# Softmax attention on one core: when the numerator products of the first exponential tile are issued

## The chip, the cores and the metric

The kernel runs on one NeuronCore of one Trainium2 chip. The metric is the device time of one launch in microseconds (us). Engines are named as the profile names them: PE is TensorE, PEld its weight loads, DVE is VectorE, ACT is ScalarE, POOL is GpSimd, SP is SyncE.

## What is computed

Four layers follow each other on x of shape 8 x 512 x 512: a cosine attention, a ternary feed-forward block, a softmax attention and a channel mix. The change touches only the third:

```python
# x is 8 x 512 x 512 here, context 8 x 512 x 384, N_HEADS = 16, HEAD = 32
q = x @ w_q + b_q
k = context @ w_k + b_k
v = context @ w_v + b_v
scores = jnp.einsum('bqhd,bkhd->bhqk', q, k) * scale
weights = jax.nn.softmax(scores, axis=-1)
out = jnp.einsum('bhqk,bkhd->bqhd', weights, v).reshape(B, Lq, D)
return out @ w_o + b_o
```

The "numerators" are the products of exp(scores) with v before the division by the row sums.

## The kernel before

`softmax_attention` runs over 8 batches; each has four head groups (m = 0 to 3) of four heads of 32 columns. A head group is worked in 16 units u. Unit u = 4t + h is head h and key tile t of 128 keys: one score matmul of 128 keys x 512 queries (`score`, L1779), and one exponential on ACT (`exponential`, L1497) into a slot of E. Four units with the same t make one exponential tile. I call the stretch of PE's order that begins with such a tile "block t".

E has twelve slots of 512 columns for sixteen exponentials: `SLOT = (0, 4, 8, 4)`, so tile 3 takes the slots of tile 1. Before that, POOL adds tile 1 onto tile 0 and later tile 3 onto tile 2 (`summed`, L1381), and PE multiplies the sums by ones to have the softmax denominators (`denominators`, L1795).

Each engine runs its own fixed list in order, and semaphores tie the lists together. On PE each block t is, for all groups but the very last:

1. `maxima` of the next head group, query tile t (L1761): four matmuls into PSUM banks 0 to 3. They wait until ACT has read the four scores of the block before, since scores use the same banks.
2. `attend(b, m, t - 1)` (L1787): the numerators of the exponential tile before, four heads beside each other in four column groups, into the bank `NUM`. It signals `s_pv`. Block 0 instead takes tile 3 of the group before, and its first denominators.
3. In block 1 (in block 2 for m = 3) the second denominators of the group before.
4. Scores u = 4t to 4t + 3, with projections, value products, transposes and output products (`between`) put between them by tables. The scores with h = 0 and h = 2 wait (`s_red`) for DVE: it has to reduce the maxima in banks 0 and 1, then those in banks 2 and 3 (`maxima` on DVE, L1626, two instructions for each block), before the banks may be written again.

The semaphore `s_pv` has these readers that matter here. On POOL, `summed(b, m, 0, i)` waits for the numerators of tile 0 (count 16m + 4), because it writes over what they read. On ACT, the exponentials of tile 1 wait for the group before, and those of tile 3 for the numerators of tile 1 (16m + 8) and for `summed`. `attend(b, m, 0)` itself waits for `s_av`: ACT has copied the group before out of `NUM` (`numerators`, L1503). POOL's order in a group is: two sums of the group before, the low part of the next query projection, `summed(b, m, 0, 0)`, then (by m) the division remainder, the low key part, the small normalisation steps, and `summed(b, m, 0, 1)`.

Of the kernel before, what the change touches and what calls it, by code (L numbers as in the profile page):

```python
# [1183 lines left out]
def softmax_attention(env, ctx_d, bq_d, bk_d, wv_d, bv_d, wo_d, bo_d, wr_d, wkk_d, mur_d, muk_d):  # L1184
# [31 lines left out]
    with ExitStack() as ctx:  # L1216
# [78 lines left out]
        def what(b, m, first, last):  # L1295

            return (None if last and m + 2 >= NG else group(b, m, 2),
                    None if last and m + 1 >= NG else group(b, m, 1),
                    (b, m - 1) if m else None if first else (b - 1, NG - 1),
                    (b, m - 2) if m >= 2 else None if first else (b - 1, NG + m - 2))  # L1300
# [413 lines left out]
        def _(e):  # L1714
# [11 lines left out]
            def queries(b, m, w, c, bank=None):  # L1726
                bank = bank or (7 if w else q_bank(m))
                n, k, xh, xl = (("q", KD, zh, zl), ("k", KC, ch, cl))[w]
                if c == 0:
                    if m == 0:  # L1730
                        (s_zl, s_cl)[w].wait(e, b, (KD, 1)[w])
                    if bank in reader:
                        take(bank)
                    reader[bank] = (s_qkf, b, 2 * m + w + 1)
                cols = lambda x: lambda c: x[n][:, c * D + m * P:c * D + (m + 1) * P]
                last = product(banks[bank][:, :], cols(wh), cols(wl), lambda c: xh[:, c, :], lambda c: xl[:, c, :], c, k)
                if c == k - 1:
                    last.then_inc(s_p.sem, 1)

            def values(b, m, t, i=None):  # L1740
                begin = i is not None
                i = i if begin else v_bank(m)
                if t == 0 and not begin:
                    take(i)
                    reader[i] = (s_V, b, m + 1)
                rows = lambda x: lambda c: x[:, c, t * P:(t + 1) * P]
                cols = lambda x: lambda c: x["v"][:, c * D + m * P:c * D + (m + 1) * P]
                for c in range(KC):
                    last = product(banks[i][:, t * P:(t + 1) * P], rows(ch), rows(cl), cols(wh), cols(wl), c, KC)
                if t == TT - 1:  # L1750
                    last.then_inc(s_vp.sem, 1)

            def maxima(b, m, q):
                if q == 0:
                    e.wait_ge(s_qkh.sem, s_qkh.count(b, 2 * m + 2))
                    s_mrow.wait(e, b, m)
                s_red.wait(e, b, 2 * (TT * m + q))
                high = qkh[m % 2]
                for h in range(4):
                    head = slice(h * DH, (h + 1) * DH)  # L1760
                    last = e.matmul(MX[h][:, :], high[head, 0, q * P:(q + 1) * P], high[head, 1, :], start=True, stop=True)  # L1761
                last.then_inc(s_mx.sem, 1)

            def rows(b, m):
                s_ex.wait(e, b, 16 * m - 3)
                e.wait_ge(s_red.sem, s_red.count(b, 2 * TT * (m + 1)))
                e.transpose(MX[0][0:4 * TT, 0:P], mx[:, :, :].rearrange("p h q -> p (h q)"), ident[:, :]).then_inc(s_mT.sem, 1)
# [14 lines left out]
            def attend(b, m, t):  # L1782
                if t == 0:
                    s_av.wait(e, b, m)
                e.wait_ge(s_ex.sem, s_ex.count(b, 16 * m + 4 * t + 4))
                for h in range(4):
                    e.matmul(NUM[h * DH:(h + 1) * DH, :], V[:, m, t, h * DH:(h + 1) * DH], E[:, SLOT[t] + h, :],  # L1787
                             start=(t == 0), stop=(t == TT - 1)).then_inc(s_pv.sem, 1)

            def denominators(b, m, p):  # L1790
                if p == 0:
                    s_an.wait(e, b, m)
                e.wait_ge(s_sum.sem, s_sum.count(b, 4 * m + 2 * p + 2))
                for h in range(4):
                    e.matmul(DEN[h * DH:(h + 1) * DH, :], ones[:, 0:DH], E[:, SLOT[2 * p] + h, :], start=(p == 0), stop=(p == 1))\  # L1795
                        .then_inc(s_dn.sem, 1)

            def transposed(b, c, end=False):
                if c == 0:
                    s_z.wait(e, b, TT)  # L1800
                take(7)
                chunk(e, b, c, R7)
                reader[7] = (s_zh if end else s_zl, b, c + 1)

            def output(b, q, c, i=6, end=False):
                if end:
                    e.wait_ge(s_al.sem, s_al.count(b, c + 1) + (q if c == NG - 1 else 0))
                elif q == 0:
                    s_al.wait(e, b, c + 1)
                if c == 0:  # L1810
                    if i < 4:
                        e.wait_ge(s_red.sem, s_red.count(b, 2 * TT * NG))
                        e.wait_ge(s_ex.sem, s_ex.count(b, 16 * (NG - 1)))
                    else:
                        take(i)
                    reader[i] = (s_res, b, q + 1)
                rows = lambda x: lambda c: x[:, c, q * P:(q + 1) * P]
                cols = lambda x: lambda c: x["o"][:, c * D:(c + 1) * D]
                last = product(banks[i][:, :], rows(ath), rows(atl), cols(wh), cols(wl), c, NG)
                if c == NG - 1:  # L1820
                    last.then_inc(s_o.sem, 1)

            def step(b, m, first, last):
                proj, nxt, div, late = what(b, m, first, last)
                if m == 0:
                    reader[6], reader[7] = ((s_qkf, b, 3), (s_qkf, b, 4)) if first else ((s_V, b, 1), (s_V, b, 2))

                def between(u):
                    if m == 1 and u in T_AT:
                        transposed(b + 1, T_AT.index(u), last)  # L1830
                    if proj:
                        for c in range(KD):
                            if Q_AT[m][c] == u and (u >= 0 or c):
                                queries(*proj, 0, c)
                        for c in range(KC):
                            if K_AT[m][c] == u:
                                queries(*proj, 1, c)
                    if not first:
                        for q, c in O_AT[m].get(u, ()):
                            output(b - 1, q, c)  # L1840
                    for n, when in V_AT[m].items():
                        for t in range(TT):
                            if when[t] == u and not (last and m == 3):
                                values(b + (m == 3), n, t)
                    if last and m == NG - 1 and u in END_UNITS:
                        q = END_UNITS.index(u)
                        for c in range(2):
                            output(b, q, c, END_BANK[q], True)

                if proj and Q_AT[m][0] < 0:  # L1850
                    queries(*proj, 0, 0)
                rows(b, m)
                if first and m == 1:
                    e.wait_ge(s_lo, 2)
                between(-1)
                for u in range(UNITS):
                    t, h = divmod(u, 4)
                    if nxt and h == 0:
                        if t == 0:
                            s_mrow.wait(e, b, m + 1)  # L1860
                        e.wait_ge(s_ex.sem, s_ex.count(b, 16 * m + 4 * t))
                        maxima(*nxt, t)
                    if t and h == 0:
                        attend(b, m, t - 1)
                    if div and u == 0:
                        attend(*div, TT - 1)
                        denominators(*div, 0)
                    if div and u == 4 * DN_TILE[m]:
                        denominators(*div, 1)
                    between(u - 0.5)  # L1870
                    score(b, m, u, nxt)
                    between(u)
# [28 lines left out]
            first_maxima(3, 0)  # L1901
            first_maxima(3, 1)
            steps(step, e)
            denominators(B - 1, NG - 1, 0)
            for h in range(4):
# [330 lines left out]
```

## Time and profile before

| | us |
|---|---|
| median of 3 runs | 1631.55 |
| lowest and highest of them | 1624.54 and 1632.25 |
| the profiled execution, its own time | 1632.94 |
| its span in the trace | 1631.0 |
| softmax attention, first to last score | 638.7 to 1329.7 in the span |
| one batch of it in the steady loop | 86.13 |

The profiled execution's time is 1.9 us more than its span, which is what lies around the span. To read the profile for this change, one looks at one batch of the softmax stage, since six of the eight batches repeat each other, and in it at the blocks t = 1 and t = 2 of each head group: when the maxima start, when the scores can follow, and when the next maxima start. In the timelines a row is start, duration, engine, line, operation with output and inputs, count; in brackets the idle time before it and what ended it. Rows that follow each other at once on one line are merged into one with their count; a numerator block is x8, since each of its four fp32 matmuls has two passes. Starts of matmuls are as recorded; they overlap, so PE's cost of a matmul is the distance to the next start and not its duration.

### The profile page before, as it was taken

Reading aid. Unit: us, or ns where it says so; the run is one execution under the profiler, and the core shown is the slowest. Engines: PE = TensorE matmul, PEld = TensorE weight load, DVE = VectorE, ACT = ScalarE, POOL = GpSimd, SP = SyncE. Lnnn points to the kernel's source line nnn. Section 1 sums busy time; section 2 is a strip of 40 time slices with the busy share of each in tenths; the row PEclk is TensorE's granted clock in tenths of the full one; section 3 lists DMA queues with packets and bytes.
Section 4 is the critical chain, followed back from the end, with each engine's and each line's share of the span. In section 5 each row is a group of like instructions: output and inputs, shape, how many; then the busy total and the mean of one; then the engine's idle time right before and its main releaser. Section 6 shows DMA issues by size and latency. Waiting matters only on the chain. (4 is left out here: it accounts for less than half of the span.)

```text
span 1631.0 us, 28525 instructions
## 1 busy us (share of the span) xinstructions
PE 1486.4 (91%) x8732; PEld 661.3 (41%) x8732; DVE 1219.0 (75%) x1468; ACT 1114.5 (68%) x1895; POOL 1049.1 (64%) x764
## 2 busy tenths in 40 slices
PE   5999887998999987889999999999999977999898
PEld 3545433444444433334343434343434323444343
DVE  4979899988989795667686868676777767665653
ACT  6667598788888764667676667666666656665563
POOL 4777536666776735667666767677767656556662
PEclk9989999999999998999999999999999988999999
DMA  8311000000000013221211212121211112232221
GB/s 322 141 65 65 1 1 1 1 1 1 0 0 1 1 66 95 55 57 37 57 38 42 56 35 58 34 58 35 57 36 40 56 35 44 52 85 66 55 52 52
DMA packets 91706, 79.52 MB, mean 49 GB/s; under 512 B 45792, under 2 KB 71264, under 8 KB 91104
## 3 DMA queue, kind: packets, MB, share of 16 engines
q1 hardware_dynamic: 88416, 69.70, 15.3%
q10 hardware_dynamic: 3200, 8.79, 1.4%
q8 instruction: 36, 0.59, 0.2%
q14 instruction: 54, 0.44, 0.1%
HBM read 37.40 MB, written 8.39 MB: 28 GB/s over the span
## 5 line engine op out<-in xcount | busy, mean ns | idle before, releaser
L1626 DVE TENSOR_REDUCE s_mx<-bank 128x2 f32<-128x1024 f32 x248 | 291.7, 1218 | 161.0 <-PE bank L1761 160.2
L1497 ACT ACTIVATE s_E<-bank 128x512 f32<-128x512 f32 x512 | 281.3, 597 | 167.4 <-PE bank L1779 166.1
L1381 POOL TENSOR_TENSOR s_E<-s_E 128x1024 f32<-128x1024 f32 x126 | 297.9, 2375 | 83.0 <-ACT s_E L1497 82.2
L1779 PE MATMUL bank<-s_QA,s_KA 97*128 97x512 f16 x512 | 164.8, 386 | 15.9 <-DVE s_mx L1626 12.5
L1787 PE MATMUL bank<-s_E,s_V 128*32 128x512 f32 x1024 | 138.6, 614 | 4.1 <-ACT s_E L1497 2.3
L796 POOL TENSOR_TENSOR sm_wkv<-sm_wkv,sm_cx 128x511 f32<-128x511 f32 x48 | 66.0, 1375 | 91.8 <-DVE sm_wkv L986 82.4
L1099 PE MATMUL bank<-sm_zz,w1raw 128*128 128x512 f16 x256 | 100.6, 393 | 25.7 <-DVE sm_cx L986 13.3
L1122 PE MATMUL bank<-f_w2q,w2raw 128*128 128x512 f16 x512 | 121.8, 379 | 0.6 <-DVE w2raw L974 0.3
L1630 DVE RECIPROCAL bank<-bank 128x256 f32<-128x256 f32 (+1 forms) x66 | 112.7, 1708 | 8.9 <-PE bank L1795 5.4
L790 POOL TENSOR_TENSOR w1raw<-w1raw,sm_cx 128x512 f32<-128x512 f32 x88 | 115.6, 1334 | 2.3 <-ACT sm_cx L878 2.3
L1989 POOL TENSOR_TENSOR sm_cx<-m_xf,sm_cx 128x512 f16<-128x512 f32 x60 | 82.4, 1393 | 42.2 <-ACT sm_cx L2048 42.2
L1099 PE MATMUL bank<-sm_wq,w1raw 128*128 128x512 f16 x256 | 97.2, 380 | 12.0 <-DVE sm_cx L986 7.7
L1100 PE MATMUL bank<-sm_zz,w1raw 128*128 128x512 f16 x256 | 100.4, 392 | 0.0
L1100 PE MATMUL bank<-sm_wq,w1raw 128*128 128x512 f16 x256 | 97.0, 379 | 0.0
L1779 PEld LDWEIGHTS bank<-s_QA,s_KA 97*128 97x128 f16 x512 | 41.1, 97 | 115.5 <-DVE s_mx L1626 74.9
L2096 DVE SCALAR_TENSOR_TENSOR m_xf<-sm_zz,sm_mu,m_part 128x512 f32<-128x512 f32 x60 | 59.9, 1024 | 28.6 <-ACT m_part L2040 28.6
L1122 PEld LDWEIGHTS bank<-f_w2q,w2raw 128*128 128x128 f16 x512 | 50.0, 98 | 61.2 <-ACT w2raw L936 0.8
L1374 POOL TENSOR_TENSOR sm_cx<-s_qkf,sm_cx 128x512 f16<-128x512 f32 x31 | 37.8, 1220 | 57.0 <-ACT sm_cx L1475 56.6
L1374 POOL TENSOR_TENSOR sm_cx<-s_qkf,s_qkh 128x512 f16<-128x512 f32 x32 | 37.1, 1159 | 58.0 <-ACT s_qkh L1475 57.7
L2156 PE MATMUL bank<-m_wvh,m_kh 128*128 128x512 f16 x128 | 49.7, 388 | 22.7 <-DVE m_y L2112 16.8
L1722 PE MATMUL bank<-sm_wkv,sm_cx 128*128 128x128 f16 x384 | 70.2, 220 | 0.0
L1724 PE MATMUL bank<-sm_wkv,sm_cx 128*128 128x128 f16 x384 | 69.8, 220 | 0.0
(280 smaller groups left out, 4095.4 us busy)
## 6 DMA issues: line engine op xcount, KB each, us to landing
sm_cx<-in_ctx SPq DMA_DIRECT2D x16, 768.0 KB, 4.6
X<-in_x SPq DMA_DIRECT2D x8, 1024.0 KB, 6.6
s_QA<-sm_cx SPq DMA_DIRECT2D x256, 32.0 KB, 1.9
out_x<-X SPq DMA_DIRECT2D x8, 1024.0 KB, 4.5
s_KA<-sm_cx SPq DMA_DIRECT2D x244, 32.0 KB, 1.9
w1raw<-in_w ACTq DMA_DIRECT2D x1, 4096.0 KB, 15.9
w2raw<-in_w ACTq DMA_DIRECT2D x1, 4096.0 KB, 29.5
s_QA<-s_qkh SPq DMA_DIRECT2D x128, 32.0 KB, 1.8
```

Of the source, the lines that this page charges most:

```text
L790: e.tensor_tensor(o, o, s2b[:, :], ALU.mult).then_inc(s_u.sem, 1)
L1099: e.matmul(hb(odd, j), w1q[:, cols], zh(odd, c), start=(c == 0), stop=False)
L1100: last = e.matmul(hb(odd, j), w1q[:, cols], zl(odd, c), start=False, stop=(c == KD - 1))
L1122: last = e.matmul(OB[q][:, :], whole16[:, r % NQ, q * P:(q + 1) * P, 0], w2q[:, ORDER[r] * D:(ORDER[r] + 1) * D], start=False, stop=(r == ...
L1374: e.tensor_tensor(qkl[:, w, :], f, qkh[m % 2][:, w, :], ALU.subtract).then_inc(s_qkl.sem, 1)
L1381: e.tensor_tensor(into, into, other, ALU.add).then_inc(s_sum.sem, 1)
L1497: e.activation(E[:, SLOT[k] + h, :], s_bank(u, nxt)[:, :], ACT.Exp, scale=1.0 / float(np.sqrt(DH)))\
L1626: e.tensor_reduce(mx[:, 2 * i:2 * i + 2, q], MAXED[i][:, :, :], AX.X, ALU.max).then_inc(s_red.sem, 1)
L1630: e.reciprocal(DEN[:, i * n:(i + 1) * n], DEN[:, i * n:(i + 1) * n]).then_inc(s_rc.sem, 1)
L1779: e.matmul(s_bank(u, nxt)[:, :], KA[0:MROW + 1, m, h, t * P:(t + 1) * P], QA[0:MROW + 1, m, h, :], start=True, stop=True).then_inc(s_sc.se ...
L1787: e.matmul(NUM[h * DH:(h + 1) * DH, :], V[:, m, t, h * DH:(h + 1) * DH], E[:, SLOT[t] + h, :], start=(t == 0), stop=(t == TT - 1)).then_in ...
L1989: e.tensor_tensor(xl[:, i, :], xf[:, i % 3, :], xh[:, i, :], ALU.subtract).then_inc(s_xl.sem, 1)
```

## The change

In the list of PE, no numerators are issued in block 1 any more; those of tile 0 are issued in block 2, ahead of those of tile 1. Block 3 keeps those of tile 2, and block 0 of the next group those of tile 3.

```diff
-                    if t and h == 0:
-                        attend(b, m, t - 1)
+                    if h == 0:
+                        for k in ((), (), (0, 1), (2,))[t]:
+                            attend(b, m, k)
```

The lists of the other engines are as they were. On PE, block 1 of head group m = 2 in the batch loop: ahead of the change the numerators of tile 0 stand between the maxima and the denominators (s_E with s_V is a numerator product, s_E with ones a denominator product).

```order
L1761 MATMUL bank<-s_qkh 128x512 [waits s_red,s_ex]
L1761 MATMUL bank<-s_qkh 128x512 x3
L1787 MATMUL bank<-s_E,s_V 32x512 [waits s_ex,s_av]
L1787 MATMUL bank<-s_E,s_V 32x512 x3
L1793 REGISTER_ALU
L1795 MATMUL bank<-s_E,ones 32x512 [waits s_sum]
L1795 MATMUL bank<-s_E,ones 32x512 x3
L1776 REGISTER_ALU
L1779 MATMUL bank<-s_QA,s_KA 128x512 [waits s_red]
```

The same place after the change:

```order
L1761 MATMUL bank<-s_qkh 128x512 [waits s_red,s_ex]
L1761 MATMUL bank<-s_qkh 128x512 x3
L1793 REGISTER_ALU
L1795 MATMUL bank<-s_E,ones 32x512 [waits s_sum]
L1795 MATMUL bank<-s_E,ones 32x512 x3
L1776 REGISTER_ALU
L1779 MATMUL bank<-s_QA,s_KA 128x512 [waits s_red]
```

Four matmuls are gone from between the maxima and the first score of the block. Block 2 of the same group, ahead of the change, with a projection between numerators and scores:

```order
L1761 MATMUL bank<-s_qkh 128x512 [waits s_red,s_ex]
L1761 MATMUL bank<-s_qkh 128x512 x3
L1787 MATMUL bank<-s_E,s_V 32x512 [waits s_ex]
L1787 MATMUL bank<-s_E,s_V 32x512 x3
L1722 MATMUL bank<-sm_cx,sm_wkv 128x512
L1723 MATMUL bank<-sm_cx,sm_wkv 128x512
L1724 MATMUL bank<-sm_cx,sm_wkv 128x512
L1776 REGISTER_ALU
L1779 MATMUL bank<-s_QA,s_KA 128x512 [waits s_red]
```

And after it:

```order
L1761 MATMUL bank<-s_qkh 128x512 [waits s_red,s_ex]
L1761 MATMUL bank<-s_qkh 128x512 x3
L1787 MATMUL bank<-s_E,s_V 32x512 [waits s_ex,s_av]
L1787 MATMUL bank<-s_E,s_V 32x512 x3
L1787 MATMUL bank<-s_E,s_V 32x512 [waits s_ex]
L1787 MATMUL bank<-s_E,s_V 32x512 x3
L1722 MATMUL bank<-sm_cx,sm_wkv 128x512
L1723 MATMUL bank<-sm_cx,sm_wkv 128x512
L1724 MATMUL bank<-sm_cx,sm_wkv 128x512
L1776 REGISTER_ALU
L1779 MATMUL bank<-s_QA,s_KA 128x512 [waits s_red]
```

The four matmuls and the wait for s_av now stand here, ahead of the block's first score. All 32 head groups are changed in this way.

## Rows read from the trace of the kernel before

**Rows 1.** The page, busy time (share of the span) and instructions of each engine.

```profile
PE 1486.4 (91%) x8732; PEld 661.3 (41%) x8732; DVE 1219.0 (75%) x1468; ACT 1114.5 (68%) x1895; POOL 1049.1 (64%) x764
```

**Rows 2.** Busy time by stretch: head group 1 of batch 4, and the batch's sum.

```profile
1006.10:1028.89 22.79, 21.70 (x137) 8.43 (x137) 18.36 (x20) 15.77 (x30) 14.68 (x9) 1.00 0.14 35
...
sum 86.13, PE 83.63 PEld 34.37 DVE 62.97 ACT 58.43 POOL 60.48; mean PE 20.91 PEld 8.59 DVE 15.74 ACT 14.61 POOL 15.12
```

**Rows 3.** Waits in batch 4: waiter, awaited, total us, times, longest us.

```profile
PEld bank L1779 <- DVE s_mx L1626: 9.0, 15, 1.0
...
PEld bank L1761 <- ACT s_E L1497: 4.2, 10, 0.7
```

**Rows 4.** Timeline of PE, batch 4, m = 1, blocks 1 and 2.

```profile
1011.20 0.39 PE L1761 MATMUL bank<-sm_cx 32*128 32x512 f16 x4
1011.53 1.07 PE L1787 MATMUL bank<-s_E,s_V 128*32 128x512 f32 x8
1012.41 1.04 PE L1795 MATMUL bank<-s_E,ones 128*32 128x512 f32 x8
1013.38 0.60 PE L1779 MATMUL bank<-s_QA,s_KA 97*128 97x512 f16 x2
...
1014.47 0.60 PE L1779 MATMUL bank<-s_QA,s_KA 97*128 97x512 f16 x2
...
1016.30 0.40 PE L1761 MATMUL bank<-sm_cx 32*128 32x512 f16 x4
1016.62 1.07 PE L1787 MATMUL bank<-s_E,s_V 128*32 128x512 f32 x8
1017.62 0.39 PE L1722 MATMUL bank<-s_woh,s_ath 128*128 128x512 f16 x1
...
1021.86 0.40 PE L1761 MATMUL bank<-sm_cx 32*128 32x512 f16 x4
```

**Rows 5.** Timeline of DVE and of ACT, same group, block 1.

```profile
1011.72 2.36 DVE L1626 TENSOR_REDUCE s_mx<-bank 128x2 f32<-128x1024 f32 x2 [0.81 <-PE bank L1761]
...
1013.89 2.17 ACT L1497 ACTIVATE s_E<-bank 128x512 f32<-128x512 f32 x4 [1.63 <-PE bank L1779]
```

**Rows 6.** Timeline of PE and DVE, batch 4, m = 0, blocks 1 and 2.

```profile
990.81 0.39 PE L1761 MATMUL bank<-s_qkh 32*128 32x512 f16 x4
...
995.76 0.39 PE L1761 MATMUL bank<-s_qkh 32*128 32x512 f16 x4
...
998.69 0.61 PE L1779 MATMUL bank<-s_QA,s_KA 97*128 97x512 f16 x2
...
1000.32 0.39 PE L1761 MATMUL bank<-s_qkh 32*128 32x512 f16 x4 [0.52 <-ACT s_E L1497]
...
996.28 2.36 DVE L1626 TENSOR_REDUCE s_mx<-bank 128x2 f32<-128x1024 f32 x2
```

**Rows 7.** Timeline of PE, batch 4, m = 3, blocks 1 and 2.

```profile
1056.92 0.40 PE L1761 MATMUL bank<-sm_cx 32*128 32x512 f16 x4
...
1059.98 0.60 PE L1779 MATMUL bank<-s_QA,s_KA 97*128 97x512 f16 x2
...
1061.62 0.40 PE L1761 MATMUL bank<-sm_cx 32*128 32x512 f16 x4
...
1066.41 0.39 PE L1761 MATMUL bank<-sm_cx 32*128 32x512 f16 x4
```

**Rows 8.** Timeline of PE at the stage's end: column-group blocks back to back.

```profile
1331.74 1.04 PE L1787 MATMUL bank<-s_E,s_V 128*32 128x512 f32 x8
1332.60 1.04 PE L1909 MATMUL bank<-s_E,ones 128*32 128x512 f32 x8
```

**Rows 9.** Timeline of POOL, batch 4, m = 0: the two sums onto tile 0.

```profile
994.73 2.37 POOL L1381 TENSOR_TENSOR s_E<-s_E 128x1024 f32<-128x1024 f32 x1 [1.55 <-ACT s_E L1497]
...
999.64 2.36 POOL L1381 TENSOR_TENSOR s_E<-s_E 128x1024 f32<-128x1024 f32 x1
```

**Rows 10.** Timeline of PE in the very last head group: numerators of tile 0.

```profile
1310.86 1.93 PE L1787 MATMUL bank<-s_E,s_V 128*32 128x512 f32 x8 [1.84 <-ACT s_AT L1503]
```

## The prediction

> **What bounds the kernel now.** I read the page first: PE is busy 91% of the span, DVE 75%, ACT 68%, POOL 64% [rows 1]. Then one steady batch by stretches: of 86.13 us PE is busy 83.63, at a granted clock of 1.00, and no other engine is above 63 [rows 2]. So in this stage time is the length of PE's list plus the short waits in it. The table of waits says what those are: scores wait for DVE's reductions of the maxima, 15 times and 9.0 us in a batch, maxima wait for ACT's exponentials, 10 times and 4.2 us [rows 3]. (These are waits of the weight loads; a part of each lies under matmuls that still run, so they bound PE's idle time from above.) Last come the timelines of the blocks, because there one sees which of three things sets a block's length: PE's own list, DVE's reduction, or ACT's exponentials.
>
> The reader should see a block as a race. Time is counted from the start of the block's maxima. In block 1 of m = 1 the maxima start at 1011.20, DVE starts at 1011.72 and ends both reductions at 1014.08 [rows 4, 5]. So the first score may go at about 1.75 (one reduction is half of 2.36, so it ends at 0.52 + 1.18 = 1.70, and 0.05 for the signal) and the third at 2.88 + 0.05 = 2.93. The 0.05 is read in block 2 of m = 0: the reductions end at 996.28 + 2.36 = 998.64, the third score starts at 998.69 [rows 6]. Now to what PE does meanwhile: numerators 0.88, denominators 0.97, and it comes to the first score at 2.18 and to the third at 3.27 [rows 4]. PE is late for DVE by 0.34 at the third score, so this block is bound by PE's list. Its numerators are thus the cover under which DVE reduces, and only the top 0.34 us of them is on the path.
>
> **What the change takes from block 1.** The four matmuls of the numerators leave, 0.88 us where denominators follow, about 1.00 where another product follows (1016.62 to 1017.62 [rows 4]). But the third score can't go before 2.93. So:
> - m = 1: third score from 3.27 to 2.93. What follows it in PE's list is unchanged and PE-bound (the next maxima start without a wait), so the block goes from 5.10 to 4.77: minus 0.33.
> - m = 0: the same list up to the third score. The block is 4.95 long [rows 6]; minus 0.33 gives 4.62. The exponentials allow 4.56: in block 2 of m = 0 the next maxima come 1000.32 - 998.69 = 1.63 after the third score, and are released by ACT [rows 6], so 2.93 + 1.63 = 4.56 is the floor of any block. 4.62 is just above: minus 0.33.
> - m = 2 has the list of m = 1 in block 1: minus 0.33.
> - m = 3: the third score goes at 3.06 (1059.98 - 1056.92) and the block is 4.70 [rows 7], which is 3.06 + 1.64: here ACT ends it. It falls to the floor: minus 0.13.
>
> Sum for a batch: minus 1.12 us. The bounds: it can't be above zero in length, and can't be more than the whole of the products, 3 x 0.88 + 1.00 = 3.6; I take 1.12, since the DVE rows stand in these very blocks.
>
> **What the change adds to block 2.** A second column-group block right behind the first. The trace has no two numerator blocks behind each other, but numerators with denominators behind them at the stage's end, 1331.74 to 1332.60, 0.86 apart, and 0.88 in block 1 [rows 8, 4]. I take 0.86; the upper bound is 1.00, that of a block alone. There it meets no slack of the reductions, for PE already has a full list ahead of the scores:
> - m = 1: nothing in this block waits before the next maxima, it is 5.56 long (1016.30 to 1021.86 [rows 4]) and carries the transposes of the next batch. Their chain (PE transpose, ACT copy, DVE remainder, next transpose) starts behind the first score and moves as a whole: plus 0.86.
> - m = 2 and m = 3: PE's list sets the third score (in m = 3 it stands later than 2.93 and the block is 4.79 [rows 7]); a later third score moves all that follows: plus 0.86 each.
> - m = 0: the third score waits for DVE (2.93), and the next maxima wait 0.52 for ACT [rows 6]. PE comes to the third score at about 2.77, the first score and nine short value products before it; with 0.86 more, at 3.63. The block becomes 3.63 + 1.63 = 5.27 instead of 4.56: plus 0.71. So the 0.52 isn't won: ACT's exponentials move back with the score.
>
> Sum: 3 x 0.86 + 0.71 = plus 3.29 us.
>
> **What lies behind it.** Block 3 and block 0 have the same lists as before, and the waits in them (DVE in block 3 of m = 1, the maximum row at the groups' ends) hang on chains that start in block 2, so they move and don't shrink. `s_av`, for which the numerators of tile 0 wait, has come before block 1; later it costs nothing. POOL's sum onto tile 0 now waits for numerators that end 0.33 + 1.07 = 1.4 into block 2 [rows 4]. In m = 0 block 2 starts at 995.76 - 0.33 = 995.43, the numerators end at 996.8, and the first sum starts there instead of at 994.73: 2.1 later [rows 9]. Behind it on POOL wait the low key part, the normalisation steps and the second sum, which then ends at 999.64 + 2.36 + 2.1 = 1004.1. The first exponential that needs it (u = 14) would start near 1004.5 in the new timing, the third score of block 3 at 1004.0 plus 0.5. That is a margin of 0.4 us, the narrowest; in m = 1 to 3 fewer steps stand between the two sums. I cost it at nothing.
>
> **The sum.** A steady batch: 3.29 - 1.12 = 2.17 us, on 86.13. Six of the eight batches are steady: 13.0. The first batch has no output products and its first group waits for DVE anyway; in the last batch the lists are thinner too, and in the very last group the numerators of tile 0 now wait 1.84 us for ACT [rows 10], which the move removes, while the doubled block costs it back in the next. I take half a batch for each, an estimate: 2 x 1.1 = 2.2. Together 15.2 us. On the profiled execution that is 1632.9 + 15.2 = 1648.1; it stood 1.4 above the median, so for a median I say 1646.8, rounded 1647.
>
> **A rule against the sum.** In rows, numerators alone cost 1.00 and one that has another column block behind it 0.86 to 0.88 [rows 4, 8]. The Trainium skill, TensorEngine Tiling (Array Packing), section Tiling Modes, says that changing the tiling mode drains TensorE, so grouping blocks of one mode should save drains. By that rule the merged blocks are a gain, and the trace agrees on the sign and shows its size, about 0.13. It is the first rival.
>
> **Rivals.**
> 1. *Not slower: PE's list alone decides.* If block 1 weren't held by the reductions, the change would only join two column-group blocks and save 1.00 - 0.87 = 0.13 in each of 31 groups: minus 4 us, 1628. It decides at the third score of block 1: it would have to go before 2.93. Against it: DVE's reductions take 2.36 from the same start whatever PE does [rows 5], and the third score of block 2 of m = 0 stands right behind them with the fill gone [rows 6].
> 2. *Waits elsewhere give it back.* If the later waits don't move with block 2, up to 0.77 in block 3 of m = 1 and as much at a group's end may be absorbed: 2.17 - 1.5 = 0.6 for a batch, 5 us in all, 1637. For it: PE's idle time in a batch is 86.13 - 83.63 = 2.5 us. Against: the chains named above.
> 3. *POOL becomes the bound.* If the sums take longer than in [rows 9] or the margin of 0.4 in m = 0 isn't there, exponential u = 14, then maxima and scores, wait for POOL. At the worst the whole 2.1 us shift passes to the path in one group of each batch: 8 x 2.1 = 17 more, 1664.
> 4. *The doubled block costs more than 0.86*, up to 1.00 in each group: 31 x 0.14 = 4 more, 1651; this lies within the range of the forecast.
>
> **How the numbers follow.** Forecast (with rival 4): 0.80, between 1641 and 1654, by an error of a third in the batch's 2.17 and by the first and last batch. Rival 1: 0.04. Rival 2: 0.08. Rival 3: 0.08. The forecast's own range holds about 0.75; stretched a little to both neighbours, 1639 to 1656 holds 8 in 10. About 0.5%, 8 us, is what a measurement can tell from no change: above 1639.7 is slower, with 0.88 (forecast and rival 3); within 0.5% is rival 2 and most of rival 1, 0.10; faster 0.02.
>
> **What would show it.** In the timeline of a steady batch: in block 1 the third score 2.93 after the maxima in all four groups, directly behind the second reduction, and blocks of 4.77, 4.62, 4.77 and 4.57; in block 2 x16 numerators of some 1.9 us, and blocks longer by 0.86 (0.7 in m = 0); a batch of 88.3 us; in the table of waits more for scores behind DVE. Block 3 lengths unchanged would refute rival 2; exponentials that wait for POOL's sums would show rival 3. The forecast is wrong if the batch is 86 us, or if a single block carries several us.

## The result and the profile after

| | before | after |
|---|---|---|
| median of the timed runs, us | 1628.05 | 1647.14 |
| lowest and highest, us | 1623.82 and 1632.25 | 1644.50 and 1647.36 |
| span of the profiled execution, us | 1631.0 | 1642.6 |
| first maxima of the softmax stage in it, at us | 636.8 | 629.5 |
| from there to the end, us | 994.2 | 1013.1 |
| steady batch 4, us | 86.13 | 89.10 |

The ratio of the times is 1.0116, with a 95% interval from 1.0094 to 1.0139: 19.1 us slower, where 15.2 us were forecast. The two profiled spans differ by 11.6 us only, because the layers ahead of the stage, which the change doesn't touch, took 7.3 us less in the profiled execution of after (in another profile of the same kernel they ended at 634.1). From the first maxima on, the difference is 18.9 us.

The page of after, busy time of each engine, answers to [rows 1]:

```profile
PE 1482.7 (90%) x8732; PEld 657.9 (40%) x8732; DVE 1226.7 (75%) x1468; ACT 1113.7 (68%) x1895; POOL 1046.8 (64%) x764
```

PE, ACT and POOL are busy no longer than in [rows 1]; DVE is, by 7.7 us, with the same number of instructions. The batch by stretches, against [rows 2]:

```profile
987.51:1076.61 89.10, 83.90 (x617) 34.10 (x616) 64.57 (x65) 58.33 (x109) 60.27 (x36) 1.00 0.17 45
```

(The stretch has the length of one batch and begins 0.4 ahead of the batch's first maxima, which start at 987.93.) PE is busy 83.90 us against 83.63, so 2.70 of the 2.97 us that the batch grew is idle time of PE. The table of waits of the batch (waiter, awaited, total us, times, longest) says for whom, against [rows 3]:

```profile
PEld bank L1779 <- DVE s_mx L1626: 13.3, 17, 2.1
...
PEld bank L1761 <- ACT s_E L1497: 4.3, 10, 0.7
```

Scores wait 4.3 us more for the reductions (9.0 before), maxima as long as before for ACT. The longest wait, 2.1, wasn't there. Now the timeline of PE, m = 1, blocks 1 and 2, against [rows 4]:

```profile
1013.83 0.39 PE L1761 MATMUL bank<-sm_cx 32*128 32x512 f16 x4
1014.15 1.06 PE L1795 MATMUL bank<-s_E,ones 128*32 128x512 f32 x8
1016.43 0.61 PE L1779 MATMUL bank<-s_QA,s_KA 97*128 97x512 f16 x2 [1.21 <-DVE s_mx L1626]
...
1017.56 0.61 PE L1779 MATMUL bank<-s_QA,s_KA 97*128 97x512 f16 x2
...
1019.39 0.40 PE L1761 MATMUL bank<-sm_cx 32*128 32x512 f16 x4
1019.72 1.92 PE L1787 MATMUL bank<-s_E,s_V 128*32 128x512 f32 x16
1021.57 0.39 PE L1722 MATMUL bank<-s_woh,s_ath 128*128 128x512 f16 x1
...
1025.81 0.39 PE L1761 MATMUL bank<-sm_cx 32*128 32x512 f16 x4
```

Block 2: two numerator blocks stand as x16 behind the maxima and cost 1021.57 - 1019.72 = 1.85, where one cost 1.00; the block is 6.42 long, 0.86 more than before. Block 1: the numerators are gone, PE stands still for 1.21 ahead of the first score, and the third comes at 3.73 from the maxima, not at 2.93. The block is 5.57 long, where it was 5.10 and 4.77 was forecast.

All the blocks, as distances between the maxima of the timeline:

| us | blocks 1, m = 0 to 3 | blocks 2, m = 0 to 3 | batch |
|---|---|---|---|
| before | 4.95, 5.10, 5.10, 4.70 | 4.56, 5.56, 4.89, 4.79 | 86.13 |
| forecast | 4.62, 4.77, 4.77, 4.57 | 5.27, 6.42, 5.75, 5.65 | 88.3 |
| after | 4.62, **5.57**, 4.76, 4.58 | 5.29, 6.42, 5.75, 5.65 | 89.10 |

Blocks 0 and 3 have kept their lengths within 0.03 (in block 3: 5.78, 7.03, 5.20 and 5.44). Seven of eight terms fell within 0.02. One is off by 0.80, and it has to do with DVE. The timeline of DVE in after, end of block 0 and block 1 of m = 1:

```profile
1009.24 2.36 DVE L1626 TENSOR_REDUCE s_mx<-bank 128x2 f32<-128x1024 f32 x2 [2.83 <-PE bank L1761]
1011.51 3.72 DVE L156 TENSOR_SCALAR s_z<-X,s_mv,s_rstd 128x512 f32<-128x512 f32 x4
1015.16 2.34 DVE L1626 TENSOR_REDUCE s_mx<-bank 128x2 f32<-128x1024 f32 x2
```

The same place before, where the four normalisations of the next batch's rows (`normalise`, L156) stand ahead of the reductions of block 1:

```profile
1008.89 2.02 DVE L156 TENSOR_SCALAR s_z<-X,s_mv,s_rstd 128x512 f32<-128x512 f32 x4
```

They take 3.72 instead of 2.02. Nobody waited: it is the instructions themselves that are longer. Grouped by line, after and then before (count, shortest, median and longest in ns):

```profile
L156 DVE TENSOR_SCALAR s_z<-X,s_mv,s_rstd x4: 532/537/2355, 1011.5 to 1014.7; 128x512 f32<-128x512 f32 x4
```

```profile
L156 DVE TENSOR_SCALAR s_z<-X,s_mv,s_rstd x4: 533/536/651, 1008.9 to 1010.4; 128x512 f32<-128x512 f32 x4
```

One of four takes 2.36 us instead of 0.54 to 0.65. In every batch but the first it is the first of the four, with 2.09 to 2.36; in the first batch that one takes 1.17. DVE then starts the reductions of block 1 late. What does POOL do at that time? Its timeline in after, m = 0 to m = 1, and before:

```profile
999.42 2.36 POOL L1381 TENSOR_TENSOR s_E<-s_E 128x1024 f32<-128x1024 f32 x1 [4.04 <-PE bank L1787]
1004.25 2.35 POOL L1381 TENSOR_TENSOR s_E<-s_E 128x1024 f32<-128x1024 f32 x1
1007.67 1.27 POOL L1430 TENSOR_TENSOR X<-X,s_bo 128x512 f32 x1
1008.89 4.69 POOL L1381 TENSOR_TENSOR s_E<-s_E 128x1024 f32<-128x1024 f32 x2
```

```profile
1004.58 4.67 POOL L1381 TENSOR_TENSOR s_E<-s_E 128x1024 f32<-128x1024 f32 x2
```

The first sum of m = 0 waits for the numerators that moved, and everything behind it on POOL moves too, as the prediction had it for the sums onto tile 0. Counted from the batch's first maxima (985.71 before, 987.93 after), the first sum starts at 11.49 instead of 9.02, 2.5 later where 2.1 was forecast. But it goes on to the sums onto tile 2. Before, they ended at 1009.25, when DVE had just begun its normalisations; now they end at 1013.58, and DVE's long instruction at 1013.87. Counted from the first maxima again, these sums run 2.1 later, and DVE reaches its normalisations only 0.4 later.

### The profile page after: what moved, and what is told of

Its sections match the earlier page's. It is cut to its first block and busy times, and to the rows that moved or that the text cites. A ratio compares the mean times of both kernels' runs of the same rounds, so it can differ in the third digit from the quotient of the medians.

```text
span 1642.6 us, 28525 instructions
## 1 busy us (share of the span) xinstructions
PE 1482.7 (90%) x8732; PEld 657.9 (40%) x8732; DVE 1226.7 (75%) x1468; ACT 1113.7 (68%) x1895; POOL 1046.8 (64%) x764
## 5 line engine op out<-in xcount | busy, mean ns | idle before, releaser
L1787 PE MATMUL bank<-s_E,s_V 128*32 128x512 f32 x1024 | 132.3, 612 | 1.5 <-ACT s_E L1497 1.5
L1722 PE MATMUL bank<-sm_wkv,sm_cx 128*128 128x128 f16 x384 | 69.8, 220 | 0.0
L1724 PE MATMUL bank<-sm_wkv,sm_cx 128*128 128x128 f16 x384 | 69.4, 219 | 0.0
L1723 PE MATMUL bank<-sm_wkv,sm_cx 128*128 128x128 f16 x384 | 69.3, 219 | 0.0
L2041 ACT ACTIVATE m_part<-sm_zz,sm_omu 128x512 f32<-128x512 f32 x60 | 42.6, 711 | 37.6 <-POOL sm_zz L2003 34.8
```

## The experiments

The theory: (a) blocks 1 and 2 grow and shrink by the terms of the sum, a pure loss of cover for the reductions; (b) the 0.80 of block 1 of m = 1 comes from POOL's sums that now run beside DVE's normalisations. Rivals: the 0.80 belongs to the moved products themselves; the loss is the doubled column block or its place and would come with any fill.

**The changed kernel again**, with its batches as the yardstick on this chip.

> The changed kernel again, beside the kernel before and the three variants, as their common base. Theory A (two causes): PE's list costs 2.2 us a batch as forecast, and 0.8 us more a batch come from block 1 of head group m = 1, where the first of DVE's four normalisations takes 2.36 us instead of 0.65, because it meets POOL's sums. Expected 16 to 20 us above before; batches of 89.1 us.

1647.31 against 1627.84, ratio 1.0128 (1.0108 to 1.0148), and a batch of 89.09 with the same blocks (5.56 in the one in question). The result repeats. (The ratios and intervals here and below are those on record; they are not the quotients of the two medians, which would be 1.0120 here.)

**POOL's order alone, on the changed kernel.** POOL's small normalisation steps in m = 0 go ahead of the sum that waits, and the bias of tile 0 (L1430) goes into m = 1:

```diff
+                if m == 1:
+                    bias(b, 0)
+                if m == 0:
+                    ln_p(e, b + 1)
...
-                if m == 0:
-                    ln_p(e, b + 1)
...
-                e.tensor_tensor(tile(b, m), tile(b, m), bo[:, :], ALU.add).then_inc(s_bo.sem, 1)
+                if m:
+                    bias(b, m)
```

> The changed kernel with POOL's list alone reordered: in m = 0 the two small normalisation steps go ahead of the first sum (POOL is idle there for 4 us), and the bias addition of m = 0 goes behind the low query part of m = 1. The last two sums of group 0 then start some 2.2 us sooner against DVE's normalisations. Theory A (the extra 0.8 us a batch is a meeting of DVE and POOL): first normalisation back to about 0.6 us, block 1 of m = 1 back from 5.57 to 4.77, batch 88.3, so 5 to 6 us less than the changed kernel, 12 to 14 above before. Rival B (the extra comes from PE's or DVE's own order, not from when POOL runs): block 1 of m = 1 stays at 5.57, no change to the changed kernel.

The timeline of DVE:

```profile
1009.93 2.36 DVE L1634 TENSOR_REDUCE s_mx<-bank 128x2 f32<-128x1024 f32 x2 [2.83 <-PE bank L1769]
1012.21 1.91 DVE L156 TENSOR_SCALAR s_z<-X,s_mv,s_rstd 128x512 f32<-128x512 f32 x4
1015.04 2.36 DVE L1634 TENSOR_REDUCE s_mx<-bank 128x2 f32<-128x1024 f32 x2 [0.92 <-PE bank L1769]
```

and of POOL:

```profile
1007.71 4.68 POOL L1381 TENSOR_TENSOR s_E<-s_E 128x1024 f32<-128x1024 f32 x2
```

The sums end at 1012.39, just as the normalisations begin; these take 0.54 to 0.55 each, and DVE waits for PE again. The maxima rows of m = 1:

```profile
1014.52 0.39 PE L1769 MATMUL bank<-sm_cx 32*128 32x512 f16 x4
1019.28 0.40 PE L1769 MATMUL bank<-sm_cx 32*128 32x512 f16 x4
1025.70 0.39 PE L1769 MATMUL bank<-sm_cx 32*128 32x512 f16 x4
```

Block 1 is 4.76, the forecast's 4.77, block 2 stays at 6.42, and the batch is 88.29, the forecast's 88.3. So 0.81 of a batch is (b) and 2.16 is (a). The median, 1644.46 (ratio 1.0113, 1.0095 to 1.0132), lies only 2.9 us under the changed kernel, where six batches give 0.80 x 6 = 4.8 and 5 to 6 were expected. The two intervals overlap, so the saving is shown by the blocks and not by the timed runs.

**The same order in the kernel before**, as a control.

> The kernel before with POOL's list reordered as in the second variant (normalisation steps ahead of the first sum, the bias addition of m = 0 in m = 1). A control: in the kernel before no normalisation is held, so the order on POOL is worth nothing. Theory A: batch 86.1 and a time within 2 us of before. If POOL's order is worth something by itself: several us either way.

1626.30 against 1628.06, ratio 0.9997 (0.9982 to 1.0013), batch 86.11. POOL's order is worth nothing where its sums didn't meet the normalisations.

**A late POOL in the kernel before**, with PE's list untouched. Two bias additions are brought forward to m = 0 and hold POOL up:

```diff
-                e.tensor_tensor(tile(b, m), tile(b, m), bo[:, :], ALU.add).then_inc(s_bo.sem, 1)
+                for q in ((0, 1, 2), (), (), (3,))[m]:
+                    e.tensor_tensor(tile(b, q), tile(b, q), bo[:, :], ALU.add).then_inc(s_bo.sem, 1)
```

> The kernel before with PE's list untouched; POOL's bias additions of tiles 1 and 2 are made in m = 0 with that of tile 0, so POOL reaches the last two sums of group 0 about 2.5 us later and they run while DVE comes to its normalisations. Theory A: the first normalisation is held until one of the sums ends (at the latest 2.9 us after it could start), DVE's reductions of block 1 in m = 1 start up to 2 us late, of which 0.34 us is covered, and the kernel is 4 to 12 us slower though nothing on PE moved. If DVE gets in between the two sums, it is held 0.6 us only and the time is unchanged within 2 us. Rival B: no change at all, and normalisations of 0.65 us.

DVE's timeline:

```profile
1008.71 2.36 DVE L1627 TENSOR_REDUCE s_mx<-bank 128x2 f32<-128x1024 f32 x2 [2.83 <-PE bank L1762]
1010.99 5.05 DVE L156 TENSOR_SCALAR s_z<-X,s_mv,s_rstd 128x512 f32<-128x512 f32 x4
1015.96 2.34 DVE L1627 TENSOR_REDUCE s_mx<-bank 128x2 f32<-128x1024 f32 x2
```

POOL's:

```profile
1005.44 3.73 POOL L1431 TENSOR_TENSOR X<-X,s_bo 128x512 f32 x3
1009.12 4.88 POOL L1381 TENSOR_TENSOR s_E<-s_E 128x1024 f32<-128x1024 f32 x2
1014.50 1.25 POOL L1374 TENSOR_TENSOR sm_cx<-s_qkf,s_qkh 128x512 f16<-128x512 f32 x1 [0.51 <-ACT s_qkh L1476]
```

The normalisations take 5.05: in their order 0.79, 2.58, 0.54 and 1.38. The last of them lies beside POOL's low key part (L1374), so it isn't the sums alone that stretch them. The only block that changes is again block 1 of m = 1: 6.89 instead of 5.10. The batch is 87.93, 1.8 more, and the kernel 1640.82, ratio 1.0084 (1.0062 to 1.0105): 13 us slower, where 4 to 12 were expected, with nothing moved on PE and no load on the engine that bounds. This is the effect (b) by itself, and larger than in the changed kernel.

**The numerators of tile 1, not of tile 0, moved by one block.** Here block 1 is left alone and block 2 loses its cover to block 3.

```diff
-                    if t and h == 0:
-                        attend(b, m, t - 1)
+                    if h == 0:
+                        for k in ((), (0,), (), (1, 2))[t]:
+                            attend(b, m, k)
```

> The kernel before with another pair joined: the numerators of tile 0 stay in block 1, those of tile 1 move from block 2 to block 3, ahead of those of tile 2. The same number of matmuls, the same joining of two column blocks, another place. Theory A (what counts is what DVE's reductions and ACT's exponentials leave free in the two blocks), worked from the rows of the kernel before: block 2 goes from 4.56, 5.56, 4.89, 4.79 (m = 0 to 3) to 4.56, 5.38, 4.76, 4.58, together 0.5 less; block 3 from 5.78, 7.03, 5.23, 5.44 by plus 0.86, plus 0.1 (it waits 0.77 for DVE already), plus 0.86 and plus 0.7, together 2.5 more. So 2.0 us a batch, batch 88.1, about 14 us slower than before. POOL's first sum isn't late here, so the normalisations stay at 0.65 us. Rival C (the loss of the changed kernel is special to tile 0: its readers on POOL, its wait for ACT's copy): then this kernel is within 3 us of before.

1643.91 against 1628.06, ratio 1.0107 (1.0087 to 1.0127), 16 us where 14 were expected; batch 87.98, where 88.1 was expected. Blocks 2 are 4.56, 5.39, 4.77 and 4.56, blocks 3 are 6.64, 7.03, 6.05 and 6.13. The normalisations are short (1.91 for four), as POOL's first sum isn't delayed. The account of (a) thus carries over to another pair of blocks. One term was 0.1 too large: block 3 of m = 1 didn't grow at all. Its rows:

```profile
1025.63 0.40 PE L1761 MATMUL bank<-sm_cx 32*128 32x512 f16 x4
1025.96 1.92 PE L1787 MATMUL bank<-s_E,s_V 128*32 128x512 f32 x16
...
1032.66 0.40 PE L1761 MATMUL bank<-s_qkh 32*128 32x512 f16 x4
```

7.03 long with x16 in it as with x8: a block that is bound by a chain (here DVE's step for the next batch) takes a second column block for nothing. In after, no block 2 was of that kind.

**Other cover for block 1.** If the loss is missing cover, other products of block 2 can be put into block 1. Tables that place key projections, value products and output products are changed, so that one piece of each m goes from block 2 into block 1. An entry is the score behind which a piece is issued, or with a half ahead of the next one: 3.5 to 7 are block 1, 7.5 to 11 block 2. In m = 0 and 2 the piece at 7.5 goes to 7 and the one at 7 to 3.5, in m = 1 the one at 7.5 goes to 3.5, and in m = 3 those at 9, 7 and 5 go to 7, 5 and 3.5:

```diff
-    K_AT = ((3, 5, 7), (5, 7, 7), (7, 7.5, 11), (3, 3.5, 5))
-    V_AT = ({2: (7, 7.5, 9, 11), 3: (11.5, 11.5, 13, 15)}, {}, {}, {0: (7, 7, 9, 11), 1: (11, 11.5, 13, 15)})
+    K_AT = ((3, 5, 7), (5, 7, 7), (3.5, 7, 11), (3, 3.5, 3.5))
+    V_AT = ({2: (3.5, 7, 9, 11), 3: (11.5, 11.5, 13, 15)}, {}, {}, {0: (5, 7, 7, 11), 1: (11, 11.5, 13, 15)})
...
-    O_AT = ({}, {3: ((0, 0),), 7.5: ((0, 1),), 9: ((0, 2),),
+    O_AT = ({}, {3: ((0, 0),), 3.5: ((0, 1),), 9: ((0, 2),),
```

> The changed kernel with other products put where the numerators of tile 0 were: in each head group one piece (0.5 or 0.65 us of PE) that stood in block 2 is issued in block 1 ahead of a score. Theory A (the numerators were cover for DVE's reductions, and any product can be the cover): block 2 shortens by 0.5 to 0.65 us in each group while block 1 grows by 0.13 at most, together 2.0 to 2.2 us a batch, so 12 to 15 us less than the changed kernel, which leaves it 3 to 7 us above before (the part with POOL stays, and in m = 1 it hides the cost of the piece). Rival C (the numerators themselves are dear where they are now, by array mode or by their waits): at most a third of that comes back.

1637.45, ratio 1.0068 (1.0048 to 1.0087), batch 87.64: 1.45 us of a batch and some 10 us of the kernel came back without touching the numerators; 2.0 to 2.2 and 12 to 15 were expected. Blocks 1 are 4.62, 5.80, 4.89 and 4.58, blocks 2 are 4.79, 6.13, 5.10 and 5.65. In m = 1, block 2 shortened by 0.29 only, but block 3 by 0.36 as well, to 6.67. Block 2 of m = 3 gained nothing, and block 1 of m = 1 is again too long (5.80): this kernel keeps POOL's order. There the lines show how the two engines meet. DVE and POOL:

```profile
1008.61 3.96 DVE L156 TENSOR_SCALAR s_z<-X,s_mv,s_rstd 128x512 f32<-128x512 f32 x4
```

```profile
1006.51 4.86 POOL L1381 TENSOR_TENSOR s_E<-s_E 128x1024 f32<-128x1024 f32 x2
```

The first normalisation takes 0.55, at about the place where POOL's first sum ends (1006.51 + 2.4 = 1008.9), the second 2.58 and ends at 1011.66, 0.29 after the second sum.

**The same tables in the kernel before**, as a control.

> The kernel before with the same pieces moved from block 2 to block 1 as in the fourth variant, the numerators left where they were. A control for whether that move is worth something by itself. Theory A: block 1 is bound by PE's list and grows by the whole piece in m = 0 to 2, block 2 can't fall below 4.56: 5 to 9 us slower than before. If the move is good by itself, it is faster than before.

1644.10, ratio 1.0107 (1.0083 to 1.0132), batch 88.17, and 5 to 9 us were expected where 16 came. The blocks 1 are 5.46, 5.75, 5.75 and 5.25: overfull, each longer than before (4.95, 5.10, 5.10, 4.70), while blocks 2 hardly fall (4.56, 5.40, 4.77 and 4.79, where 4.56, 5.56, 4.89 and 4.79 stood). I had sized m = 3 wrong: three projection pieces stand there. So the same move that returned 10 us in one kernel costs 16 in the other; it is no gain of its own, it fills the hole that the change left.

**POOL's order and the fill together**, with the second denominators of m = 3 moved into block 1 as well:

```diff
-    DN_TILE, AN_AT = (1, 1, 1, 2), 12
+    DN_TILE, AN_AT = (1, 1, 1, 1), 12
```

> The changed kernel with both repairs: POOL's order, and the pieces of block 2 put in block 1 as cover; for m = 3 the second denominators go from block 2 to block 1 as well, since there the scores of block 2 stood behind three column blocks. Theory A: block 1 of 4.62, 4.9, 4.89, 4.8 and block 2 of 4.79, 6.1, 5.10, 4.8; batch 86.2 to 86.5, time 0 to 3 us above before. If the joined numerators cost something of their own, it stays above before by more than 5 us.

1631.87, ratio 1.0025 (1.0009 to 1.0040), 3.8 us above before where 0 to 3 were expected, batch 86.55. Block 1 of m = 3 became 5.25, for which 4.8 was expected: with three pieces and the denominators PE comes late to the scores, and of the 0.86 that block 2 wins (4.79 for 5.65) 0.67 is spent here (5.25 for 4.58).

**The same without the overfull block**: POOL's order and the output products as above, but in m = 3 the denominators only go into block 1.

```diff
-    K_AT = ((3, 5, 7), (5, 7, 7), (7, 7.5, 11), (3, 3.5, 5))
-    V_AT = ({2: (7, 7.5, 9, 11),
+    K_AT = ((3, 5, 7), (5, 7, 7), (3.5, 7, 11), (3, 3.5, 5))
+    V_AT = ({2: (3.5, 7, 11, 11),
```

> The changed kernel refitted: POOL's order as in the second variant, one piece of block 2 put in block 1 for m = 0, 1, 2, and for m = 3 the second denominators alone (the former variant had three pieces there, and its block 1 was 5.25). In m = 0 one value product goes from ahead of the third score of block 2 to behind the fourth. Theory A: block 1 of 4.62, 4.9, 4.89, 4.70; block 2 of 4.58, 6.1, 5.10, 4.79; batch 85.8 against 86.1 of before, so a time 0 to 4 us under before. If the joined numerators had a cost of their own, it could not fall to before.

1628.39 against 1627.50, ratio 1.0005 (0.9993 to 1.0018), batch 86.05. Blocks 1 are 4.62, 4.89, 4.89 and 4.70, blocks 2 are 4.79, 6.13, 5.10 and 4.79. With the joined numerators and all else fitted to them the kernel is as fast as before within the interval, and not faster. The level isn't reached in blocks 1 and 2 alone, which together are still 0.26 longer than before (39.91 against 39.65); it needs block 3 of m = 1, which is 6.66 instead of 7.03. The wait ahead of its first score, before and in x9_refit:

```profile
1024.61 0.39 PE L1779 MATMUL bank<-s_QA,s_KA 97*128 97x512 f16 x1 [0.77 <-DVE s_mx L1626]
```

```profile
1018.64 0.39 PE L1787 MATMUL bank<-s_QA,s_KA 97*128 97x512 f16 x1 [0.40 <-DVE s_mx L1634]
```

So a part of the price was paid back by a wait that the fill shortened, and not by cover in block 1. I expected 85.8, from a 4.58 in block 2 of m = 0 that stayed at 4.79; why it did isn't settled. Nothing that ran beats the kernel before.

## Why the prediction was right, and where it was off

The sign and the mechanism held, and the loss was 19.1 us where 15.2 were forecast. That the times agree to 0.1 us (1647.14 and 1647) is luck: the forecast stood on a median of before of 1631.55, which came out as 1628.05 in the comparison, 3.5 lower, and its loss was 3.9 too small.

1. *Block 1 shrinks to the reductions, not by the products' time.* Right. 4.62, 4.76 and 4.58 where 4.62, 4.77 and 4.57 were forecast, and 4.76 for the last once POOL is out of the way.
2. *Block 2 grows by 0.86, and by 0.71 in m = 0.* Right: 0.86 in three of them and 0.73. Two joined column blocks cost 1.85, so the second costs 0.85.
3. *Blocks 3 and 0 keep their waits.* Right, which refutes rival 2. In x5_late3 a block with such a wait did absorb a column block, because there the products went into it; so the rival's mechanism exists, at another place. In x4_fill and x9_refit that wait of block 3 did shrink, from 0.77 to 0.40 in the latter, so it isn't fixed either.
4. *POOL: "I cost it at nothing".* This is the step that failed. I followed the delay of 2.1 us (2.5 in the trace) down POOL's list to the second sum onto tile 0 and asked only who waits for it: exponential u = 14. It waits for nothing, as I had said. But the delay doesn't end there. It reaches the two sums onto tile 2 (in front of them nothing waits long enough to swallow it: before they began at 1004.58, after at 1008.89), and these now lie beside DVE's four normalisations, the first of which then lasts until the sums are over. What the two engines contend for is in no row. Price: 0.80 in a batch, 4.7 in six (item 5), shown by taking it away (x1_pool) and by making it alone (x3_before_delay). Rival 3 named the right engine and the right 2.1 us, with the wrong route and price.
5. *Six steady batches: 13.0 us; first and last batch: 2.2 us.* The steady batches cost more, the ends about what was forecast. The six batches took 535.57 instead of 516.78, 18.8 more, but 1.0 of that is one batch (batch 1) that took 90.11 in this execution and 89.09 in x0_after, the same program, whose six batches took 534.5: 17.7 more, the forecast's 13.0 and 4.7 for step 4. The first batch went from 90.40 to 90.08, which says nothing, as this batch took anything from 87.48 to 93.05 in the traces of the kernels here, and 89.19 in x0_after. Its blocks 1 and 2 of m = 1 to 3, which are steadier, add up to 28.87 before and 30.29 after: plus 1.4. The last batch, up to its last maxima, took 57.86 (56.26 before): plus 1.6. In the very last group, which has no maxima, the 1.84 of [rows 10] is gone. The timeline of PE in after, from that group's start to its numerators of tile 2:

```profile
1317.79 1.07 PE L1787 MATMUL bank<-s_E,s_V 128*32 128x512 f32 x8 [0.28 <-ACT s_E L1497]
...
1325.46 0.59 PE L1779 MATMUL bank<-s_QA,s_KA 97*128 97x512 f16 x1 [1.92 <-ACT s_E L1497]
...
1327.88 3.64 PE L1787 MATMUL bank<-s_E,s_V 128*32 128x512 f32 x16
...
1337.64 1.06 PE L1787 MATMUL bank<-s_E,s_V 128*32 128x512 f32 x8 [1.22 <-ACT s_E L1497]
```

The way is 19.85; before, the same two rows stood at 1305.00 and 1325.43, 20.43 apart. So the move gave back 0.6 and not 1.84: PE now waits for ACT ahead of block 1's four scores instead, 0.26, 0.71, 1.92 and 1.29, where the last two waited 0.34 and 1.00 and the first two not at all. (The granted clock is the lower level, 1.2 GHz, for most of this place in both kernels: 0.51 on average from 1310 to 1320 before, 0.66 from 1323 to 1333 after. Two numerator blocks cost 3.41 there.) The ends together are thus 1.4 + 1.6 - 0.6 = 2.4, where 2.2 was forecast.
6. *Rival 1.* Refuted, and it was priced too high as well. It took 0.13 for each joined pair, but in m = 0 to 2 the move also parts a pair. Before, numerators and denominators cost 1013.38 - 1011.53 = 1.85 together and the other numerators 1.00 [rows 4]; after, two numerators cost 1.85 and the denominators are left alone. What these cost alone shows in x9_refit, where no wait follows them:

```profile
1005.56 1.06 PE L1803 MATMUL bank<-s_E,ones 128*32 128x512 f32 x8
1006.56 0.39 PE L1730 MATMUL bank<-s_woh,s_ath 128*128 128x512 f16 x1
```

They cost 1.00, and the sum is 2.85 both times. Only in m = 3, where all three column blocks now follow each other, something is saved. After:

```profile
1066.27 1.92 PE L1787 MATMUL bank<-s_E,s_V 128*32 128x512 f32 x16
1068.02 1.04 PE L1795 MATMUL bank<-s_E,ones 128*32 128x512 f32 x8
1068.99 0.39 PE L1779 MATMUL bank<-s_QA,s_KA 97*128 97x512 f16 x1
```

That is 2.72 for 2.85. So joining was worth 0.13 for a batch and about 1 us in all, not 4, against the 19 that the change costs; in x9_refit so little can't be told from nothing.

The Trainium skill, SBUF — State Buffer, section Who interferes with whom, has a rule that bears on step 4: DVE and GpSimd share a pair of ports to the on-chip memory, the instruction that is issued first holds it to its end and the other engine blocks, `tensor_scalar` can run in modes that need the pair and `tensor_reduce` never contends on this chip. The runs agree: in before, after, x3_before_delay and x4_fill only the normalisations (TENSOR_SCALAR) were stretched, up to 2.67 us beside sums of 2.36, and the reductions, some of them beside the same sums, stayed at 2.34 to 2.36 for two. Which port mode the normalisations ran in no run here shows.

## What to carry to other kernels

Price a moved instruction at both places: where it leaves, by what it hides (here a reduction that takes 2.36 us in any case), and where it lands, by whether anything there still waits. Then follow the delay of each engine that waits for it through its whole list, and ask not only who waits for that engine but also whose instructions it will now run beside. The stretched instruction showed in no table of waits here; compare the longest with the median of a line.

## What was unexpected of the hardware

- A DVE normalisation of 128x512 in fp32 takes 0.54 us alone. One that begins while POOL adds a 128x1024 tile ends 0.3 us after that sum, wherever in the sum it began (unless its own 0.54 us last longer, as in x1_pool, where it begins 0.17 ahead of the end): it took 2.07 to 2.67 us when it began at the sum's start or up to 0.6 into it, and 0.65 in the kernel before, where it begins 0.36 ahead of the sum's end. Ends of the normalisation and the sum: 1013.87 and 1013.58 in after, 1011.66 and 1011.37 in x4_fill, 1014.27 and 1013.99 in x3_before_delay. Beside POOL's shorter L1374 (1.25 us, in x3_before_delay) one took 1.38.
- With two POOL sums behind each other, one normalisation can get in between them, and the next is held for all of the second: 0.55 and 2.58 in x4_fill, 0.79 and 2.58 in x3_before_delay. POOL pays little: two sums take 4.67 alone, 4.69 in after, and 4.86 and 4.88 in the two kernels where one got in.
